# Second layer's experts run only for the chosen token-expert pairs, sorted through HBM by indirect transfers, with logits placed behind the transposes

## The reference

```python
scores = softmax(xt @ gate_w.T); biased = scores + gate_b
idx = top_k(biased, 2)                       # 2 of 8 experts for each token
cw = sum(one_hot(idx, 8) * weights[..., None], axis=1)
h1 = einsum('td,efd->etf', xt, w1) + b1;  h3 = einsum('td,efd->etf', xt, w3) + b3
a = swiglu(h1 * h3)                          # g*sigmoid(1.702 g)*(l+1), g and l clipped
y = einsum('etf,edf->etd', a, w2) + b2
routed = einsum('te,etd->td', cw, y)         # six of eight weights are zero
shared = swiglu((xt @ sw1.T + sb1) * (xt @ sw3.T + sb3)) @ sw2.T + sb2
```

## Time and profile before

| | us |
|---|---|
| median of 3 executions | 1907.16 |
| lowest, highest | 1906.37, 1907.27 |
| profiled execution, its own time | 1911.44 |
| span of the profiled execution, first to last instruction | 1909.6 |
| mean granted TensorE clock in it (1 = 2.4 GHz) | 0.895 |
| PE, VectorE, ACT, POOL busy in it | 1586.4, 1444.9, 938.4, 596.7 |

### The profile page before, as it was taken

How to read it: one execution, slowest core, us unless ns; L and a number is a source line. 1 busy time by engine, 2 the same in 40 slices (tenths; PEclk the granted TensorE clock), 3 DMA queues, 4 the chain that set the end, 5 groups by cost and what they waited for, 6 DMA issues and landing times. The chain is left out here.

```text
span 1909.6 us, 42021 instructions
## 1 busy us (share of the span) xinstructions
PE 1586.4 (83%) x15322; PEld 1026.0 (54%) x15322; DVE 1444.9 (76%) x3721; ACT 938.4 (49%) x2029; POOL 596.7 (31%) x598
## 2 busy tenths in 40 slices
PE   1277777767469299999999999999998379999996
PEld 0177777666444245555555555555555265555553
DVE  6699999997569646666666666666666727999999
ACT  1455555554210226666666666666665123444442
POOL 3486666661113315111211211121100303333332
PEclk7688888888679589999999999999999659999998
DMA  1000000000000012111111111111100000000001
GB/s 67 0 1 1 1 1 1 1 1 0 12 1 1 17 18 40 29 27 28 32 29 26 31 30 26 30 31 28 28 20 9 20 1 2 13 8 14 7 7 45
DMA packets 100092, 32.50 MB, mean 17 GB/s; under 512 B 91186, under 2 KB 92228, under 8 KB 99780
## 3 DMA queue, kind: packets, MB, share of 16 engines
q1 hardware_dynamic: 99332, 30.07, 8.5%
q10 hardware_dynamic: 576, 0.07, 0.0%
HBM read 15.43 MB, written 2.10 MB: 9 GB/s over the span
## 5 line engine op out<-in xcount | busy, mean ns | idle before, releaser
L1135 DVE TENSOR_REDUCE ntop<-score 128x1 f32<-128x512 f32 x512 | 318.2, 684 | 253.7 <-PE score L1016 253.7
L1094 ACT ACTIVATE prob<-score,ntop 128x512 f32<-128x512 f32 x512 | 317.7, 687 | 270.8 <-DVE ntop L1135 270.8
L371 ACT ACTIVATE hist<-zp 128x168 f32<-128x168 f32 (+1 forms) x768 | 224.1, 313 | 171.3 <-DVE zp L340 170.6
L1052 PE MATMUL turned<-ident,prob 128*128 128x128 f32 x2048 | 268.5, 280 | 1.4 <-DVE probT L1078 1.4
L421 PEld LDWEIGHTS py<-hist,diagC 128*128 128x128 f32 x2048 | 262.9, 214 | 0.0
L421 PE MATMUL py<-hist,diagC 128*128 128x128 f32 x2048 | 262.7, 297 | 0.0
L1016 PE MATMUL score<-ks,qs 64*128 64x512 f32 x1024 | 257.6, 622 | 0.0
L1052 PEld LDWEIGHTS turned<-ident,prob 128*128 128x128 f32 x2048 | 219.0, 141 | 49.4 <-issue 27.4
L391 POOL TENSOR_TENSOR xb<-xc,Bm 128x1024 f32<-128x1024 f32 x128 | 244.9, 1952 | 1.3
L335 DVE TENSOR_TENSOR gp<-hist,Ap 128x168 f32<-128x168 f32 (+1 forms) x768 | 231.1, 331 | 14.7 <-POOL xb L391 14.7
L340 DVE TENSOR_TENSOR zp<-gp,xb 128x168 f32<-128x168 f32 (+1 forms) x768 | 234.7, 336 | 0.0
(11 more groups left out here) (236 smaller groups left out, 1934.0 us busy)
## 6 DMA issues: line engine op xcount, KB each, us to landing
tb<-in_table SPq DMA_DIRECT2D x64, 127.1 KB
rel_q<-q_sb SPq DMA_DIRECT2D x256, 8.0 KB
ks<-k_sb SPq DMA_DIRECT2D x32, 128.0 KB
key_q<-q_sb SPq DMA_DIRECT2D x248, 8.0 KB
w<-in_ew SPq DMA_DIRECT2D x9, 320.0 KB, 2.8
x<-in_x SPq DMA_DIRECT2D x1, 2048.0 KB, 8.8
q_sb<-cm SPq DMA_DIRECT2D x64, 32.0 KB
k_sb<-inv SPq DMA_DIRECT2D x64, 32.0 KB
```

The lines of the kernel that those rows point to most:

```text
L371: nc.scalar.activation(hist[:, par, u, lo:hi], zp[j][:, 0:hi - lo], ACT.Tanh)\
L1052: last = nc.tensor.transpose(turned_ps[BANK[e]][:, j * P:(j + 1) * P], prob[G % 2][e][:, j * P:(j + 1) * P], ident[:, :])
L1094: nc.scalar.activation(prob[G % 2][e][:, :], score_ps[r][:, :], ACT.Exp, bias=ntop[:, G % 2, e:e + 1]).then_inc(prob_ready, 1)
L1135: v.tensor_reduce(ntop[:, G % 2, e:e + 1], score_ps[r][:, :], AX.X, ALU.max, negate=True)\
```

## The change

- **Logits follow transposes.** `Normed.tensor` takes a function `follow`; behind the transposes of block j PE runs the logits of block j-1, in `experts0` and `experts1`. Both wait for their small inputs ahead of the transposes now. The norm's semaphores are made once for all three norms, with offsets.
- **Only chosen pairs.** Each token has 2 of 8 experts, 8192 pairs. They are sorted by expert into blocks of 256 rows, each expert's share rounded up: 32 + 7 = 39 blocks (`RB`). PE counts the pairs ahead of each pair (`spots`: 34 matmuls into one bank, with a triangular matrix and the ones, whose moving columns are 256, 8, 248, then 248, 240, ... down to 8), VectorE makes from it the row of each pair (`pos`), the expert of each block (`eid`) and the block's biases (`bsel`).
- **Sorting.** POOL scatters the 32 tiles of the normed `h`, once for each of the two choices: 64 indirect DMAs of 128 rows of 512 bytes into `sorted_h` in HBM. The scan stage fills that tensor (5.1 MB) with zeros.
- **Steps.** 16 shared steps of 256 tokens come first, then the 39 routed ones, 55 in all. For a routed step SP loads 256 rows of `sorted_h` and the 320 KB of the block's expert (into one of three buffers, its number read from SBUF into a register), PE turns the rows (`turn`), ACT copies them, and the result is copied by ACT (`take`) and stored by SP into `sorted_y`. VectorE clips now. `G3` and `L3` have one buffer instead of two.
- **Collecting.** When all 39 blocks are stored, POOL gathers 64 times 128 rows of `sorted_y`, and VectorE adds them with their weights to `acc` (`combine`), scales, adds to `x` (`finish`).

The core of the diff (buffers, semaphores and the arithmetic of positions on small tiles left out):

```diff
+PARTS = 1
+PT = NT // PARTS
+SLOTS = 2 * P
+HALVES = SLOTS // P
+NSHARED = NB * SEQ // SLOTS
+RB = 2 * PT * P // SLOTS + NE1 - 1
+NROUTED = PARTS * RB
+MOST = PT * P // SLOTS
...
+            sp.wait_ge(nought_set, 1)
+            for s in range(PARTS):
+                sp.dma_start(hs[s].rearrange("(n p) e -> p n e", p=P),
+                             nought[:, :].unsqueeze(1).to_broadcast([P, RB * HALVES, P])).then_inc(hs_zeroed, 16)
...
+            if follow and j:
+                pe.wait_ge(self.hT_ready, self.all0 + j)
+                follow(j - 1)
+        if follow:
+            pe.wait_ge(self.hT_ready, self.all0 + NBLK)
+            follow(NBLK - 1)
...
+    NW, NX, NY, NGOT = 3, 4, 4, 8
+    N = NSHARED + NROUTED
+    AFTER = 3
...
+            sp.dma_start(Wsh[:, :], d["ew1"][NE1:NALL, :, :].rearrange("o p n -> p (o n)")).then_inc(shared_in, 16)
+            sp.wait_ge(eid_ready, 1)
+
+            def load_weights(m):
+                if m >= NW:
+                    sp.wait_ge(y_ready, NSHARED + m - NW + 1)
+                e = sp.value_load(eid[0:1, m:m + 1], min_val=0, max_val=NE1)
+                sp.dma_start(W[m % NW][:, :], d["ew1"][bass.ds(e, 1), :, :].rearrange("o p n -> p (o n)"))\
+                  .then_inc(routed_in[m % NW], 16)
+
+            def load_slots(m):
+                if m % RB == 0:
+                    sp.wait_ge(scattered[m // RB], 16 * 2 * PT)
+                if m >= NX:
+                    sp.wait_ge(xs_turned, m - NX + 1)
+                sp.dma_start(xs[m % NX][:, :, :],
+                             hs[m // RB][m % RB * SLOTS:(m % RB + 1) * SLOTS, :].rearrange("(o p) e -> p o e", o=HALVES))\
+                  .then_inc(xs_in[m % NX], 16)
+
+            def store(m):
+                sp.wait_ge(y_taken, NSHARED + m + 1)
+                sp.dma_start(ys[m // RB][m % RB * SLOTS:(m % RB + 1) * SLOTS, :].rearrange("(o p) e -> p o e", o=HALVES),
+                             ysb[m % NY][:, :, :]).then_inc(y_out[m % NY], 16)
+
+            load_slots(0)
+            for m in range(NROUTED):
+                if m + 1 < NROUTED:
+                    load_slots(m + 1)
+                load_weights(m)
+                if m >= AFTER:
+                    store(m - AFTER)
+            for m in range(NROUTED - AFTER, NROUTED):
+                store(m)
...
+            for s in range(PARTS):
+                for k in range(s * PT, (s + 1) * PT):
+                    for r in range(2):
+                        g.indirect_dma_start(out=hs[s][:, :], out_offset=bass.IndirectOffsetOnAxis(ap=pos[:, r, k:k + 1], axis=0),
+                                             in_=norm.h[:, k, :], in_offset=None).then_inc(scattered[s], 16)
+            for s in range(PARTS):
+                for i in range(NY):
+                    pool.wait_ge(y_out[i], 16 * stores(i, (s + 1) * RB))
+                for k in range(s * PT, (s + 1) * PT):
+                    if k >= NGOT:
+                        pool.wait_ge(got_in[k % NGOT], 32 * (k // NGOT))
+                        pool.wait_ge(combined, 2 * (k - NGOT) + 2)
+                    for r in range(2):
+                        g.indirect_dma_start(out=got[:, k % NGOT * 2 + r, :], out_offset=None, in_=ys[s][:, :],
+                                             in_offset=bass.IndirectOffsetOnAxis(ap=pos[:, r, k:k + 1], axis=0))\
+                         .then_inc(got_in[k % NGOT], 16)
...
+            def slots(n):
+                m = n - NSHARED
+                act.wait_ge(xs_turned, m + 1)
+                A.copy(xT[:, m % 2, :], XT[m % 2][:, 0:SLOTS]).then_inc(xT_ready, 1)
...
+            def take(n):
+                act.wait_ge(y_ready, n + 1)
+                if n < NSHARED:
+                    dst = acc[:, n * HALVES:(n + 1) * HALVES, :]
+                else:
+                    m = n - NSHARED
+                    if m >= NY:
+                        act.wait_ge(y_out[m % NY], 16 * (m // NY))
+                    dst = ysb[m % NY][:, :, :]
+                A.copy(dst.rearrange("p o e -> p (o e)"), Y[n % 2][:, 0:SLOTS]).then_inc(y_taken, 1)
...
+            for n in range(N + 2):
+                if NSHARED <= n + 1 < N:
+                    slots(n + 1)
+                if n < N:
+                    if n == NSHARED:
+                        act.wait_ge(eid_ready, 2)
+                    gate(n)
+                if 1 <= n <= N:
+                    tanh(n - 1)
+                if n < N:
+                    lin(n)
+                if n >= 2:
+                    take(n - 2)
...
+            v.tensor_tensor(chosen[:, :, :], hot[0][:, :, :], hot[1][:, :, :], ALU.add).then_inc(chosen_ready, 1)
...
+                chain(v.tensor_tensor(keys[:, :, :], hot[r][:, :, :], spot[:, :, :], ALU.mult))
+                chain(v.tensor_reduce(posf[:, r, :], keys[:, :, :], AX.X, ALU.add))
+            v.tensor_copy(pos[:, :, :], posf[:, :, :]).then_inc(pos_ready, 1)
...
+            def gates(n):
+                q = n % 2
+                dve.wait_ge(first_g, n + 1)
+                v.scalar_tensor_tensor(gg[:, q, :], G3[:, 0:SLOTS], bias(n, 2), g1[:, q, :], ALU.add, ALU.mult)\
+                 .then_inc(gg_raw, 1)
+                dve.wait_ge(gg_raw, n + 1)
+                v.tensor_scalar(gg[:, q, :], gg[:, q, :], LIMIT, LOWEST, ALU.min, ALU.max).then_inc(gg_ready, 1)
...
+            def combine(k):
+                dve.wait_ge(got_in[k % NGOT], 32 * ring(k, NGOT))
+                for r in range(2):
+                    v.scalar_tensor_tensor(acc[:, k, :], got[:, k % NGOT * 2 + r, :], wt[:, r, k:k + 1], acc[:, k, :],
+                                           ALU.mult, ALU.add).then_inc(combined, 1)
+                    dve.wait_ge(combined, 2 * k + r + 1)
...
+            LATE = NSHARED + RB + AFTER + 2
+            for n in range(N + 1):
+                if n < N:
+                    gates(n)
+                if n >= 1:
+                    join(n - 1)
+                if n < N:
+                    lins(n)
...
+            for k in range(min(PT, max(0, N + 1 - LATE)), NT):
+                combine(k)
+                if k % TPB == TPB - 1:
+                    finish(k // TPB)
...
+            norm.tensor(pe, logits)
+            pe.wait_ge(consts, CONSTS)
+            pe.wait_ge(chosen_ready, 1)
+            spots = SPOTS[:, 0:PARTS * (PT + 1) * NE1].rearrange("p (s k e) -> p s k e", s=PARTS, e=NE1)
+            picked = chosen[:, :, :].rearrange("p (s k) e -> p s k e", s=PARTS)
+            for s in range(PARTS):
+                flat = lambda t: t.rearrange("p k e -> p (k e)")
+                mm(flat(spots[:, s, 0:PT, :]), tri[:, :], flat(picked[:, s, :, :]), start=(s == 0), stop=False)
+                mm(flat(spots[:, s, PT:PT + 1, :]), ones[:, :], flat(picked[:, s, PT - 1:PT, :]), start=False, stop=False)
+                for by in range(1, PT + 1):
+                    to = PT if by == 1 else PT + 1
+                    last = mm(flat(spots[:, s, by:to, :]), ones[:, :], flat(picked[:, s, 0:to - by, :]),
+                              start=False, stop=(s == PARTS - 1 and by == PT))
+            last.then_inc(spots_ps, 1)
...
+            def turn(n):
+                m = n - NSHARED
+                pe.wait_ge(xs_in[m % NX], 16 * ring(m, NX))
+                if m >= 2:
+                    pe.wait_ge(xT_ready, m - 1)
+                for o in range(HALVES):
+                    last = nc.tensor.transpose(XT[m % 2][:, o * P:(o + 1) * P], xs[m % NX][:, o, :], ident[:, :])
+                last.then_inc(xs_turned, 1)
...
+                    w, src = W[m % NW], xT[:, m % 2, :]
+                    pe.wait_ge(routed_in[m % NW], 16 * ring(m, NW))
+                    pe.wait_ge(xT_ready, m + 1)
...
+            def down(n):
+                w = Wsh if n < NSHARED else W[(n - NSHARED) % NW]
+                if n == 0:
+                    pe.wait_ge(shared_half, 1)
                 pe.wait_ge(a_ready, n + 1)
-                if not (isinstance(n, int) and n < 2):
-                    pe.wait_ge(y_summed, n - 1)
-                for t in range(TPB):
-                    last = mm(Y[j % 2][:, t * P:(t + 1) * P], a[:, j % 2, t * P:(t + 1) * P],
-                              W[p][:, 4 * P:5 * P], start=True, stop=True)
+                if n >= 2:
+                    pe.wait_ge(y_taken, n - 1)
+                for o in range(HALVES):
+                    cols = slice(o * P, (o + 1) * P)
+                    if n < NSHARED:
+                        k = n * HALVES + o
+                        mm(Y[n % 2][:, cols], cwT[:, k * P:(k + 1) * P], b2[:, :], start=True, stop=False)
+                    last = mm(Y[n % 2][:, cols], a[:, n % 2, cols], w[:, 4 * P:5 * P],
+                              start=(n >= NSHARED), stop=True)
                 last.then_inc(y_ready, 1)
 
-            def body(e, p):
-                pe.wait_ge(we_in[p], weights_in(e, p))
-                for j in range(NBLK):
-                    n, q = e * NBLK + j, j % 2
```

(82 more changed lines are left out.)

390 lines of the change are left out of this document (211 added, 179 removed).

## The result

The changed kernel takes 2062.95 us (median of 4 runs, 2061.46 to 2069.28) against 1907.22 before: a ratio of **1.082, with a 95% interval of 1.081 to 1.084**. It is 156 us slower; the forecast was +92.

What follows compares the result with a forecast made beforehand. In the experts PE was busy without a gap at full clock, VectorE at 94%. Logits, selection, scatter, ring-paced routed steps and gathers summed to E+466 = 2001.4 us against 1909.6, +92, or 1999 for the median; range 1885 to 2110.

Steps and rivals of the forecast that it cites:

- 1. Logits: Logits following the transposes in both expert stages: 7.0 us less in each, together -14.0 us.
- Forecast E: End of the second logits, 1549.4 us before and 1535.4 forecast; E+n counts us from there.
- 2. Selection: Selection and places behind the logits: `chosen` E+9.1, PE's counting 12.4 us, `pos` E+25.4, VectorE's first step E+31.0.
- 3. Shared steps: 16 shared steps at VectorE's 2.7 us, PE needing 2.6 at full clock: 43 us, ending at E+74.
- 4. Scatter: 64 indirect scatters on POOL at 1.1 us, 70 us, plus 10 beside VectorE's steps and 2 for landing: E+108.
- 5. Routed steps: 36 routed periods of 7.2 us (5.3 to 8.9), paced by the weights' ring: 259 us, ending at E+382.
- D: Rival: PE at 1.2 GHz in every routed step, period 8.3, and in part of the shared ones; 2046 us; chance 0.15.
- 6. Collecting: Last routed block out about 8 us, 64 gathers 70 us, end 6 us: E+466, 2001.4 us.
- C: Rival: VectorE's steps hold the scatter back 26 us, not 10; an indirect DMA takes 1.5 us; 2066 us; chance 0.15.
- B: Rival: an indirect DMA takes 0.7 us on POOL, routed period 5.3 us; 1872 us, 1870 for the median; chance 0.16.
- E (loads ahead): Rival: the weights' ring is no stall, 36 routed steps at 2.7 us; about 1837 us; chance 0.03.
- A: The forecast itself: both indirect passes bare, weight loads pace the routed steps; +92 us, 1999 for the median; chance 0.50.

Runs made afterwards that it cites:

- experiment 2: Changed kernel with SP reading the expert number before its wait for the down projection, not after; 2039.94 us, 1.070.
- Experiment 3: Changed kernel with seven extra 256-column products, result unused, behind 36 of the routed down projections to keep PE busy; 1988.48 us, 1.043.
- experiment 1: Changed kernel with five weight buffers instead of three, nothing else; 1910.93 us, 1.002.
- experiment 11: Changed kernel with five weight buffers, weights and tokens each loaded one step earlier, expert number read before the wait; 1863.64 us, 0.978.
- 6: 5 plus blocks of tokens loaded two steps ahead and the expert number read ahead (five token, seven store buffers); 1880.37 us, 0.986.
- 5: Changed kernel with five weight buffers, stores issued five steps behind instead of three, eight store buffers, four gather buffers; 1882.9 us, 0.987.
- 7: 6 with the tokens sorted in two halves, each with its own scatter and gather; 1882.89 us, 0.987.
- 8: Changed kernel without the second choices' 32 scatters; 2055.02 us, 1.077.
- 9: The kernel of 6 once more, on another chip; 1880.01 us, 0.985.
- 10: The kernel of 8 once more, on another chip; 2054.38 us, 1.076.
- 12: The kernel of experiment 11 with four gather buffers instead of eight; 1861.95 us, 0.977.

## Why the prediction was right in its sign, and what was off

The mechanism stood: both indirect passes lie bare, and the weights' ring, with nothing ahead, paces the routed steps. Against the forecast's span of 2001.4 us the profiled one has 66 more (64 by the medians). By the steps of the prediction:

- **1. Logits.** Forecast E = 1535.4, measured 1532.9. The stage itself gave 7.0 us as said, `experts0` 6.1; the attention stages took 2.6 and the scan 0.9 less, for which I had nothing (the kernel before varies by as much from run to run). Alone, the edit gave 11.7, which its interval doesn't tell from 14.
- **2. Selection.** `chosen` at E+8.7 (said 9.1), `spots` about 12.2 us (12.4), `pos` handed over at E+25.9 (25.4). Right, the estimate of when the clock comes back included.
- **3. Shared steps.** 3.39 us apart, not 2.7, at full clock. PE's timeline of one step:

```profile
1574.54 0.60 PE L1685 MATMUL pz<-hTz,w_shared 128*128 128x256 f32 x2
...
1575.84 0.59 PE L1694 MATMUL pz<-hTz,w_shared 128*128 128x256 f32 x2
...
1576.36 0.48 PE L1707 MATMUL pz<-b,cwT 9*128 9x128 f32 x2
1576.77 0.49 PE L1708 MATMUL pz<-w_shared,a 128*128 128x128 f32 x2
...
1577.19 0.48 PE L1707 MATMUL pz<-b,cwT 9*128 9x128 f32 x2
...
1577.61 0.49 PE L1708 MATMUL pz<-w_shared,a 128*128 128x128 f32 x2
...
1577.93 0.60 PE L1685 MATMUL pz<-hTz,w_shared 128*128 128x256 f32 x2
```

The four products go as said, 0.43 each. But bias and down projection are four pairs of small products 0.41 us apart, 1.65 us where I had put 0.45 + 0.45. It cost nothing, as the scatter ends later. What cost time are the three shared steps that stand behind the turn of the first routed one: at half clock after the 32 us of waiting, their copies came at 1651, 1658 and 1665. From the scatter's landing to the first load that the ring holds back it is 27 us, and all told some 14 more than I had placed. Part of that may belong to this one execution, 6.3 us longer than the median: in the profile of experiment 2 the clock came back early and the same steps are 3.6 us apart, not 6.7.
- **4. Scatter.** Landed at E+109 (said 108), and yet by two errors that cancel: an issue costs 1.26 us, not 1.1, and of the 10 us for the lock next to nothing is there. The usual transfer takes 0.96 us with VectorE's and PE's shared steps beside it and 0.96 when both stand idle. Longer were the first two, 1.37 and 1.34, and six more beside the shared steps, 1.02 to 1.19, which is 0.6 us for the six; what made them longer is open. I had read the Trainium skill's rule too widely: "SBUF — State Buffer", Who interferes with whom, ties the lock that starves descriptor writing to VectorE's two-port modes, and says of instructions with two SBUF inputs only that they contend with GpSimd's reads. With that the trace agrees, as far as the products with two inputs go. The clips, which could run in such a mode by that section of the Trainium skill, hold the whole pass back by no more than those 0.6 us.
- **5. Routed steps.** This is the step that failed in size: 8.47 us, not 7.2, times 36, 46 us. Term by term: issue to PE 3.31 (said 2.8); from the down projection to the issue 0.73 with the read in it (said 0.3 + 0.9), the read being 0.55 by experiment 2; up and down 4.43 (said 3.2). The Trainium skill, "DMA: Bandwidth & Descriptors", Latency, has a floor of about 0.6 us for such a read, and the trace's 0.55 is near it. The mean of two clocks was the mistake. The earlier trace rows has the lower clock after a gap of 4.35 us, and the gap here is 3.7 on average, 4.0 at most: the case was D's, and I gave it 0.15. I had counted the wait and the turn as pulling in two directions and taken the middle; weighted with PE's work the clock was 0.54, hardly above its lower level.
- **6. Collecting.** 92 us from the last down projection to the end, not 84: 3.1 to the first gather (said 8), 81 for the 64 of them (said 70), 7.4 behind the last (said 6).

Together: -2.5 for E, +1.3 for the scatter, +13.8 for the left-over shared steps and what else lies between the scatter and the ring, +45.7 for the ring, +7.6 for collecting: 65.9, against the 65.8 measured. The 13.8 is what remains beside the others. Three figures of the prediction are slips that move nothing in the forecast: the period's upper bound adds up to 9.1, not 8.9; the 97 us "at PE's own pace" are 36 times VectorE's 2.7; C's time with a period of 8.3 is 2106, not 2108. Of the rivals, B (0.7 us an issue) and E (loads ahead) are out. C is out twice: next to no lock, and 1.26 instead of 1.5 us. D is what happened, on top of A: its period of 8.3 was nearly the measured one, and its 2046 falls short by the issue and the shared steps. Experiment 3 shows the clock's share, 75 us, and experiment 1 the ring's, 152 us, which holds most of the 75: between 1680 and 1810 its clock is 0.91, where the changed kernel had 0.65, and in 11, almost without gaps, it is 1.00.

The gain that was to come from fewer rows is there once the ring is open: in experiment 11 the 39 routed blocks take 103 us and 16 shared steps at 3.39 would take 54, against 332 us for the 72 steps of 512 before. Of those 175 us the gathers take back 80, bare, and the scatter 32, for which PE waits after the 53 us that lie beside shared steps.

## What to carry to other kernels

Before work is made sparse, count what paces a step when its products are gone: with a ring of three and a last reader that lags two steps, the load of each block begins only when the work it should hide behind is over. Count the wait of a store on the same queue as a lag of its own. Where every period has a gap of PE of nearly 4 us, as here, price PE's work at half speed and not at the mean of two clocks. An indirect pass of 64 transfers takes as long as some 30 routed blocks of this kernel at PE's pace, so it has to lie beside other work to be worth it.

## What the runs showed of the hardware beyond that

- An indirect DMA of 128 rows of 512 bytes costs GpSimd 0.96 us (scatter) or 0.945 (gather) and 0.30 to the next, with means of 0.98 and 0.97. Beside VectorE's shared steps six of the scatters were up to 0.2 us longer, and none once VectorE stood idle. All rows of one landed 2.2 us after its issue (scatter) or 2.5 (gather).
- The clock did not follow PE's beginning and end: it fell 1.1 us before a piece of work and came back 0.6 us after it, at 1772.6 and 1779.4. And it did not always come back at the same pace: after the same wait for the first sorted rows PE worked at 0.50 from 1644 to 1666 in the changed kernel, without idle time, while in experiment 2, where that work began at 1646, it had 0.67 from 1648 to 1652 and 1.00 from then on. In 11, where it began at 1645, it had 1.00 from 1650 on.
- Counts that PE puts on semaphores can reach ACT tens of us late while indirect transfers run: 37 us for one that ACT stood waiting for in 6, with steps of 10.4 and 10.8 us between one and the next. The profiles of 5 to 10 have it, two kernels twice, and none of the others, though 11 and 12 issue the same 64. In the stalled ones the trace also lacks most of the scatter's own landings (204 of 1,024 are there in 6, 200 in 9, all in the changed kernel and in 1, 2, 11 and 12), so that the recording of semaphores may be part of it. The Trainium skill, "NOTIFIC — the notification-queue block", Overflow, says that this block's inner pipeline holds its producers back rather than lose a record; no run here shows whether that is what happens. It wasn't tried without a profile.
